# Attention scores: three products of rounded parts, or one product in whole fp32

## The chip, the cores and the metric

The kernel runs on one core of a Trainium2 chip. The core has a matrix engine (PE, TensorE; its weight loads are shown apart as PEld), a vector engine (DVE), an activation engine (ACT), a general engine (POOL, GpSimd) and a queue that issues DMAs (SP). Each follows its own stream of instructions in order and waits on semaphores. The metric is the device time of one launch in microseconds; lower is better.

## The reference

Sixteen graphs of 512 nodes with 64 channels each, and a dense 512x512 adjacency per graph, go through four residual layers, each behind a layer norm and a relu. The change concerns the second, a graph attention:

```
h1 = tanh(x @ enc_w + enc_b)
h2 = att_layer(h1, mask, ...)      # layer 1; h3 = att_layer(h2, mask, ...) is layer 2

def att_layer(h, mask, wv, bv, wk, bk, wq, bq):
    v = tanh(h @ wv + bv)
    q = tanh(h @ wq + bq)
    k = tanh(h @ wk + bk)
    scores = einsum('bnd,bmd->bnm', q, k)
    att = softmax(scores * mask - 9e15 * (1 - mask), axis=2)
    return einsum('bnm,bmd->bnd', att, v)

z = relu(concat(h2, h3) @ w1 + b1); z = relu(z @ w2 + b2); return z @ w3 + b3
```

Layer 0 is a Chebyshev graph convolution of order 4 (three products with the adjacency), layer 2 a normalised graph convolution, layer 3 one product with the adjacency. All values are fp32.

## The kernel before

**Graphs in a pipeline.** A round works on three graphs at once: the newest (age 0) in the Chebyshev layer, the one before (age 1) in attention, the oldest (age 2) in the end of attention's second layer, the MLP, the graph convolution and the last product. There are 18 rounds: three ahead of a loop, twelve in a loop of four turns with three rounds each, three behind it. Rounds 2 to 16 have a graph in both of the first two ages. The last two have no new graph.

**Order.** A table `ORDER` lists, for each engine, the steps of a round as `step.layer-age`; `walk` (L311) issues them in that order. Nothing is scheduled otherwise: an engine that waits in one step holds all steps behind it. The steps named below are those of this table. `mask0.1-1` is the mask of row block 0 in attention layer 1, for the graph of age 1.

**Attention on the engines.** A graph's 512 nodes are four blocks of 128 rows. For each of the two layers PE makes queries, keys and values (L1009, L1014, L1021 and L1025) one after another in one PSUM bank, `qkv_ps`. ACT takes each out with a tanh (L582, L596) before PE may write the next. Queries and keys are taken out twice: once into an fp32r tile, the rounded copy (`q_hi`, `k_hi`), and once whole into `q_t`, `k_t`. POOL subtracts the two (`split_qk`, L501) into the remainders `q_lo`, `k_lo`. A score block is then three fp32r matmuls added up in PSUM (L1040, L1043, L1044): `q_hi k_hi + q_hi k_lo + q_lo k_hi`. DVE multiplies it with the adjacency (L815) and adds the bias `gate` and takes the row's extreme (L821). `gate` is made by POOL in one operation over 128x2048, for each graph and each layer (`mask_bias`, L495). ACT makes the exponential (L605), PE transposes (L1058), ACT copies (L612), PE multiplies with the values (L1075, whole fp32 operands), DVE divides (L832).

**Around layer 1.** In PE's stream stand, from one graph to the next: `queries.1`, `turn_a0` (transposes of the next graph's adjacency, L917), two transposes of probabilities, `keys.1`, `turn_a1`, `spread_inv`, `values.1`, `turn_a2`, `turn_a3`, the previous graph's `attend.2`, then the score blocks. `turn_a2` and `turn_a3` write PSUM banks that DVE must first have read in `split_at0` and `split_at1` (L729). In DVE's stream these stand behind `norm_cheb`: a product (L715) and a copy (L723) of the normalised x. In POOL's stream `norm_cheb-0` is followed by `add_cheb_bias-0` (`x_b`, L439), `split_qk.1-1` and `mask_bias.1-1`.

**Around layer 2.** POOL has `norm_gcn-2`, `mask_bias.2-1`, `split_qk.2-1`, `cheb_f0-0` (L483 to L488), `norm_last-2`, `norm_enc-0`. DVE has `gcn_fold-2`, `stats_last-2`, `mask0.2-1`, `cheb_fold1-0`, `stats_enc-0`, `norm_last-2`, and PE's last product (L955 into `post_ps`) waits for the end of that. `norm_gcn` on DVE is L846 to L745, with the product L849.

Of the kernel before, what the change touches and what calls it, by code (L numbers as in the profile page):

```python
# [21 lines left out]
F32 = mybir.dt.float32  # L22
# [5 lines left out]
P = 128  # L28
# [29 lines left out]
    "gpsimd": """  # L58
        norm_cheb-0 add_cheb_bias-0 split_qk.1-1 mask_bias.1-1 inverse_roots-0 cheb_u3-0
        norm_gcn-2 mask_bias.2-1 split_qk.2-1 cheb_f0-0 norm_last-2 norm_enc-0  # L60
        add_mlp_bias-0""".split(),
# [35 lines left out]
def graph_layers(nc, x, adj, cheb_w, cheb_b, enc_w, enc_b, att_w, att_b, w1, b1, w2, b2, w3, b3,  # L97
# [11 lines left out]
    with ExitStack() as ctx:  # L109
        def sb(name, shape, dt=F32):  # L110
            return ctx.enter_context(nc.sbuf_tensor(name, shape, dt))

        def sem(name):
# [67 lines left out]
        c_diff = sb("c_diff", [P, RB, C])  # L181
        q_t, k_t = (sb(n, [P, N]) for n in ("q_t", "k_t"))
        v_n = [sb(f"v_n{a}", [P, N]) for a in range(2)]

        q_hi, k_hi, q_lo, k_lo = (
            [sb(f"{n}{a}", [P, N], F32R) for a in range(2)]
            for n in ("q_hi", "k_hi", "q_lo", "k_lo"))
        h1_t = sb("h1_t", [P, N])
# [88 lines left out]
        f0_done = sem("f0_done")  # L277
        qkv_split = sem("qkv_split")
        rstd_done = {t: sem(f"rstd_done_{t}") for t in ("pre", "post")}
# [129 lines left out]
        def _(pool):  # L409
# [87 lines left out]

            def split(whole, high, low, g, a, k):

                pool.wait_ge(qkv_done, 10 * g.n + 5 * a + 2 * k + 2)  # L500
                gp.tensor_tensor(low[a][:], whole[:], high[a][:].bitcast(F32), ALU.subtract)\  # L501
                    .then_inc(qkv_split, 1)

            def queries_keys(g, a):
                split(q_t, q_hi, q_lo, g, a, 0)
                split(k_t, k_hi, k_lo, g, a, 1)

            def add_mlp_bias(g):
# [14 lines left out]
                "add_mlp_bias": add_mlp_bias,  # L523
                **layer(0, split_qk=queries_keys, mask_bias=mask_bias),
                **layer(1, split_qk=queries_keys),
                **layer(1, mask_bias=mask_bias),
# [4 lines left out]
        def _(act):  # L531
# [44 lines left out]

            def take(g, a, k, whole, high, bias):

                for n, to in enumerate((high[a], whole)):
                    if n and follows(g, a):  # L580
                        act.wait_ge(qkv_split, 4 * g.n + 2 * a + k - 1)
                    sc.activation(to[:], qkv_ps[:], ACT.Tanh, **bias).then_inc(qkv_done, 1)  # L582

            def queries(g, a):
                if first(g) and a == 0:
                    act.wait_ge(weights_in, 16 * n_small)
                act.wait_ge(qk_ready, 4 * g.n + 2 * a + 1)
                take(g, a, 0, q_t, q_hi, {"bias": kq_bs[a][2][:]})

            def keys(g, a):  # L590
                act.wait_ge(qk_ready, 4 * g.n + 2 * a + 2)
                take(g, a, 1, k_t, k_hi, {"bias": kq_bs[a][1][:]})

# [310 lines left out]
        def _(pe):  # L904
# [94 lines left out]
            def queries(g, a):  # L999
                if first(g) and a == 0:  # L1000
                    pe.wait_ge(weights_in, 16 * n_small)
                if a == 0:
                    pe.wait_ge(h1_done, g.n + 1)
                else:
                    pe.wait_ge(attended, 2 * g.n + 1)
                if follows(g, a):

                    pe.wait_ge(qkv_done, 10 * g.n + 5 * a)
                te.matmul(qkv_ps[:], att_ws[a][2][:], source(g, a)[:], start=True, stop=True)\  # L1009
                    .then_inc(qk_ready, 1)  # L1010

            def keys(g, a):
                pe.wait_ge(qkv_done, 10 * g.n + 5 * a + 2)
                te.matmul(qkv_ps[:], att_ws[a][1][:], source(g, a)[:], start=True, stop=True)\  # L1014
                    .then_inc(qk_ready, 1)

            def values(g, a):
                if first(g) and a == 0:
                    pe.wait_ge(bias_rows, n_bias_rows)
                pe.wait_ge(qkv_done, 10 * g.n + 5 * a + 4)  # L1020
                te.matmul(qkv_ps[:], ones_bf[:, :],  # L1021
# [11 lines left out]
            def scores_rows(g, a, i):  # L1033
                if i >= 2 or follows(g, a):

                    pe.wait_ge(masked, 8 * g.n + 4 * a + i - 1)
                part = slice(i * P, (i + 1) * P)
                if i == 0:
                    pe.wait_ge(qkv_done, 10 * g.n + 5 * a + 3)
                te.matmul(score_ps[i % 2][:], q_hi[a][:, part], k_hi[a][:], start=True, stop=False)  # L1040
                if i == 0:
                    pe.wait_ge(qkv_split, 4 * g.n + 2 * a + 2)
                te.matmul(score_ps[i % 2][:], q_hi[a][:, part], k_lo[a][:], start=False, stop=False)  # L1043
                te.matmul(score_ps[i % 2][:], q_lo[a][:, part], k_hi[a][:], start=False, stop=True)\  # L1044
                    .then_inc(scores_ready, 1)
# [25 lines left out]
            def attend(g, a):  # L1071
                pe.wait_ge(qkv_done, 10 * g.n + 5 * a + 5)
                pe.wait_ge(pt_copied, 8 * g.n + 4 * a + 4)
# [91 lines left out]
```

## Time and profile before

| | |
|---|---|
| median of 3 timed runs | 913.66 us (913.12 to 913.68) |
| the profiled execution | 909.79 us |
| its span, first to last instruction | 908.0 us |
| PE busy | 775.2 us, 85% |
| DVE busy | 593.0 us, 65% |
| ACT busy | 447.5 us, 49% |
| POOL busy | 406.3 us, 45% |
| granted PE clock, mean | 0.973 of full |
| DMA | 24 GB/s over the span |

A busy share is a mean over the span and says which engine has the least room, not what it waits for. That is read from the timeline: a row gives the start, the duration, the engine, the line and the operands; "xN" counts the instructions of the row, and the bracket gives the idle time ahead of it and who ended it. An fp32 matmul shows as two records. Ends of PE's instructions are modelled, so the pace of a stream is read from one start to the next. Rows on POOL are rough in their ends.

### The profile page before, as it was taken

How to read it: one execution, taken by the hardware profiler on the slowest of the kernel's cores; microseconds unless marked ns; L12 is line 12 of the kernel's file. 1: busy time of each engine (PE TensorE's matmuls, PEld its weight loads, DVE VectorE, ACT ScalarE, POOL GpSimd, SP SyncE). 2: the span in 40 equal slices, each digit the busy share in tenths (PEclk: the TensorE clock that was granted, in tenths of full speed). 3: DMA queues.
4: the chain of work that ended last, by engine and by line, in shares of the span. 5: the costliest groups of instructions: out<-in, count | busy, mean ns of one | idle time of the engine just before them, and what ended most of it. 6: DMA issues, size and time to landing. Idle time of an engine off the chain costs nothing. (4 is left out here: it accounts for less than half of the span.)

```text
span 908.0 us, 13130 instructions
## 1 busy us (share of the span) xinstructions
PE 775.2 (85%) x3808; PEld 542.7 (60%) x3808; DVE 593.0 (65%) x1631; ACT 447.5 (49%) x929; POOL 406.3 (45%) x491
## 2 busy tenths in 40 slices
PE   3658798989999798989979898997989899898874
PEld 2435566666667566666756666664666666675543
DVE  3265677686776668677666767766776867765432
ACT  2044646547273644737364463736465472744430
POOL 3144545445553434555443455544454455533301
PEclk9869999999999999999999999999999999999996
DMA  5000101001020200101010010102010010000000
GB/s 170 32 1 1 52 1 40 20 1 59 1 59 0 60 0 6 53 0 58 0 59 0 12 46 0 58 0 59 0 49 9 0 58 0 6 2 6 1 6 6
DMA packets 29264, 22.54 MB, mean 25 GB/s; under 512 B 19488, under 2 KB 21024, under 8 KB 29216
## 3 DMA queue, kind: packets, MB, share of 16 engines
q1 hardware_dynamic: 29216, 22.03, 8.3%
q8 instruction: 14, 0.23, 0.1%
q14 instruction: 34, 0.28, 0.1%
HBM read 19.93 MB, written 2.10 MB: 24 GB/s over the span
## 5 line engine op out<-in xcount | busy, mean ns | idle before, releaser
L605 ACT ACTIVATE negz<-negz,negmax 128x512 f32<-128x512 f32 x128 | 92.3, 721 | 96.8 <-DVE negmax L821 95.7
L425 POOL TENSOR_TENSOR rstd_post<-vareps_post,nhalf 128x4 f32<-128x4 f32 x32 | 39.1, 1221 | 196.2 <-DVE vareps_post L708 196.2
L821 DVE CUSTOM_DVE_ANT_0 negz<-negz,gate 128x512 f32<-128x512 f32 x128 | 102.7, 802 | 23.8 <-DVE negz L815 23.6
L1075 PE MATMUL turn_ps<-pt,v_n 128*128 128x512 f32 x256 | 117.4, 602 | 0.0
L425 POOL TENSOR_TENSOR rstd_pre<-vareps_pre,nhalf 128x4 f32<-128x4 f32 x32 | 34.1, 1067 | 149.5 <-DVE vareps_pre L708 149.5
L955 PE MATMUL pre_ps<-at_hi,u_pair_pre 128*128 128x512 f32 x192 | 87.4, 455 | 7.4 <-DVE u_pair_pre L745 5.2
L815 DVE TENSOR_TENSOR negz<-score_ps,a_nat 128x512 f32<-128x512 f32 x128 | 88.0, 687 | 7.6 <-PE score_ps L1044 5.3
L955 PE MATMUL post_ps<-at_hi,u_pair_post 128*128 128x512 f32 x128 | 55.8, 436 | 38.4 <-DVE u_pair_post L745 38.4
L564 ACT ACTIVATE y_t_pre<-pre_ps 128x512 f32<-128x512 f32 x48 | 28.7, 597 | 118.4 <-PE pre_ps L955 117.6
L1058 PEld LDWEIGHTS turn_ps<-ident,negz 128*128 128x128 f32 x512 | 60.9, 141 | 33.7 <-ACT negz L605 14.6
L955 PE MATMUL pre_ps<-at_lo,u_pair_pre 128*128 128x512 f32 x192 | 78.5, 409 | 0.0
L1058 PE MATMUL turn_ps<-ident,negz 128*128 128x128 f32 x512 | 75.4, 274 | 2.9 <-ACT negz L605 2.7
L1075 PEld LDWEIGHTS turn_ps<-pt,v_n 128*128 128x128 f32 x256 | 47.2, 195 | 47.3 <-issue 47.3
L612 ACT ACTIVATE pt<-turn_ps 128x512 f32<-128x512 f32 x128 | 73.8, 590 | 1.0 <-PE turn_ps L1058 0.5
L501 POOL TENSOR_TENSOR k_lo<-k_t,k_hi 128x512 fp32r<-128x512 f32 x32 | 45.8, 1432 | 57.5 <-ACT k_t L582 57.5
L917 PE MATMUL pre_ps<-ident,a_nat 128*128 128x128 f32 x256 | 42.6, 299 | 25.5 <-DVE at_lo L729 17.8
L495 POOL TENSOR_SCALAR gate<-a_nat 128x2048 f32<-128x2048 f32 x32 | 60.8, 1899 | 4.2 <-DVE negmax L821 1.6
L1040 PE MATMUL score_ps<-k_hi,q_hi 128*128 128x512 f32 x128 | 61.5, 481 | 0.4 <-DVE negz L815 0.4
L917 PEld LDWEIGHTS pre_ps<-ident,a_nat 128*128 128x128 f32 x256 | 32.4, 151 | 48.0 <-issue 32.9
L501 POOL TENSOR_TENSOR q_lo<-q_t,q_hi 128x512 fp32r<-128x512 f32 x32 | 43.7, 1366 | 31.1 <-ACT q_t L582 31.1
L832 DVE TENSOR_TENSOR h_t<-turn_ps,inv_row 128x512 f32<-128x512 f32 x32 | 22.2, 693 | 53.2 <-PE turn_ps L1075 53.2
L729 DVE TENSOR_TENSOR at_lo<-pre_ps,at_hi 128x512 fp32r<-128x512 f32 x64 | 42.7, 685 | 20.5 <-ACT at_hi L537 20.5
(138 smaller groups left out, 1838.3 us busy)
## 6 DMA issues: line engine op xcount, KB each, us to landing
a_nat<-in_adj SPq DMA_DIRECT2D x16, 1024.0 KB, 5.7
x_in<-in_x SPq DMA_DIRECT2D x16, 128.0 KB, 2.3
out<-x_out SPq DMA_DIRECT2D x16, 128.0 KB, 1.9
cheb_ws<-in_L_gnn_weight SPq DMA_DIRECT2D x2, 64.0 KB, 5.0
att_w<-in_L_gnn_a_wv SPq DMA_DIRECT2D x2, 64.0 KB, 2.7
att_w<-in_L_gnn_a_wk SPq DMA_DIRECT2D x2, 64.0 KB, 2.5
att_w<-in_L_gnn_a_wq SPq DMA_DIRECT2D x2, 64.0 KB, 2.3
bv_f<-in_L_gnn_a_bv SPq DMA_DIRECT2D x2, 64.0 KB, 2.8
```

The costliest lines, as they stand in the source:

```text
L425: gp.tensor_tensor(rstd[t][:], vareps[t][:], nhalf[:, 0:RB], ALU.pow)\
L495: gp.tensor_scalar(gate[:], a_nat[g.slot][:], -1.0, NEG, ALU.add, ALU.mult)\
L501: gp.tensor_tensor(low[a][:], whole[:], high[a][:].bitcast(F32), ALU.subtract)\
L605: sc.activation(probs[:, i, :], negz[:, i, :], ACT.Exp, bias=negmax[:, i:i + 1], scale=-1.0, accum_out=total[:, i:i + 1]).then_inc(probs_d ...
L612: sc.activation(pt[:, :, i * P:(i + 1) * P], turn_ps[i % 2][:].rearrange("p (j n) -> p j n", n=P), ACT.Copy)\
L815: ve.tensor_tensor(negz[:, i, :], score_ps[i % 2][:], a_nat[s][:, i, :], ALU.mult)\
L821: ve.tensor_tensor_reduce(negz[:, i, :], negz[:, i, :], gate[:, i, :], -1.0, 3.0e38, ALU.add, ALU.min, negmax[:, i:i + 1]).then_inc(biased, 1)
L917: mm = te.transpose(pre_ps[:, j % 2, i * P:(i + 1) * P], a_nat[g.slot][:, i, j * P:(j + 1) * P], ident[:])
L955: mm = te.matmul(bank, u_pair[t][:, j, :, :].rearrange("p a c -> p (a c)"), at[g.slot][:, j, :], start=(j == 0 and at is at_hi), stop=(j = ...
L1040: te.matmul(score_ps[i % 2][:], q_hi[a][:, part], k_hi[a][:], start=True, stop=False)
L1058: mm = te.transpose(turn_ps[i % 2][:, j * P:(j + 1) * P], probs[:, i, j * P:(j + 1) * P], ident[:])
L1075: mm = te.matmul(turn_ps[0][:], v_n[a][:, j * P:(j + 1) * P], pt[:, j, :], start=(j == 0), stop=(j == RB - 1))
```

## The change

The rounded copies `q_hi`, `k_hi` and the remainders `q_lo`, `k_lo` are gone, and with them POOL's step `split_qk` in both layers and the semaphore `qkv_split`. ACT makes one tanh each for queries and keys, into `q_t` and `k_t`, which are now two buffers each (one per layer). A score block is one matmul of the whole fp32 tiles. The semaphore `qkv_done` counts three per layer and not five. No other step changes its place in any table.

```diff
     "gpsimd": """
-        norm_cheb-0 add_cheb_bias-0 split_qk.1-1 mask_bias.1-1 inverse_roots-0 cheb_u3-0
-        norm_gcn-2 mask_bias.2-1 split_qk.2-1 cheb_f0-0 norm_last-2 norm_enc-0
+        norm_cheb-0 add_cheb_bias-0 mask_bias.1-1 inverse_roots-0 cheb_u3-0
+        norm_gcn-2 mask_bias.2-1 cheb_f0-0 norm_last-2 norm_enc-0
         add_mlp_bias-0""".split(),
...
-            def split(whole, high, low, g, a, k):
-
-                pool.wait_ge(qkv_done, 10 * g.n + 5 * a + 2 * k + 2)
-                gp.tensor_tensor(low[a][:], whole[:], high[a][:].bitcast(F32), ALU.subtract)\
-                    .then_inc(qkv_split, 1)
...
-            def take(g, a, k, whole, high, bias):
-
-                for n, to in enumerate((high[a], whole)):
-                    if n and follows(g, a):
-                        act.wait_ge(qkv_split, 4 * g.n + 2 * a + k - 1)
-                    sc.activation(to[:], qkv_ps[:], ACT.Tanh, **bias).then_inc(qkv_done, 1)
-
...
-                take(g, a, 0, q_t, q_hi, {"bias": kq_bs[a][2][:]})
+                sc.activation(q_t[a][:], qkv_ps[:], ACT.Tanh, bias=kq_bs[a][2][:]).then_inc(qkv_done, 1)
...
-                take(g, a, 1, k_t, k_hi, {"bias": kq_bs[a][1][:]})
+                sc.activation(k_t[a][:], qkv_ps[:], ACT.Tanh, bias=kq_bs[a][1][:]).then_inc(qkv_done, 1)
...
             def values(g, a):
                 if first(g) and a == 0:
                     pe.wait_ge(bias_rows, n_bias_rows)
-                pe.wait_ge(qkv_done, 10 * g.n + 5 * a + 4)
+                pe.wait_ge(qkv_done, 6 * g.n + 3 * a + 2)
...
                 if i == 0:
-                    pe.wait_ge(qkv_done, 10 * g.n + 5 * a + 3)
-                te.matmul(score_ps[i % 2][:], q_hi[a][:, part], k_hi[a][:], start=True, stop=False)
-                if i == 0:
-                    pe.wait_ge(qkv_split, 4 * g.n + 2 * a + 2)
-                te.matmul(score_ps[i % 2][:], q_hi[a][:, part], k_lo[a][:], start=False, stop=False)
-                te.matmul(score_ps[i % 2][:], q_lo[a][:, part], k_hi[a][:], start=False, stop=True)\
+                    pe.wait_ge(qkv_done, 6 * g.n + 3 * a + 2)
+                te.matmul(score_ps[i % 2][:], q_t[a][:, part], k_t[a][:], start=True, stop=True)\
                     .then_inc(scores_ready, 1)
```

On POOL, in the round's first part, `rstd_pre` and `centred_pre` are `norm_cheb`, `x_b` is the bias added to x, `q_lo` and `k_lo` are the splits, and `rs` begins the inverse roots. Before:

```order
L425 TENSOR_TENSOR rstd_pre<-vareps_pre,nhalf 128x4
L428 TENSOR_TENSOR centred_pre<-x_in,meanvar_pre 128x256
L439 TENSOR_TENSOR x_b<-x_in,cheb_bs 128x256
L501 TENSOR_TENSOR q_lo<-q_t,q_hi 128x512
L501 TENSOR_TENSOR k_lo<-k_t,k_hi 128x512
L495 TENSOR_SCALAR gate<-a_nat 128x2048
L451 TENSOR_SCALAR rs<-rs 128x4
```

POOL in the same place now:

```order
L419 TENSOR_TENSOR rstd_pre<-vareps_pre,nhalf 128x4
L422 TENSOR_TENSOR centred_pre<-x_in,meanvar_pre 128x256
L433 TENSOR_TENSOR x_b<-x_in,cheb_bs 128x256
L489 TENSOR_SCALAR gate<-a_nat 128x2048
L445 TENSOR_SCALAR rs<-rs 128x4
```

The mask's bias has moved up by two operations and stands directly behind `x_b`.

On PE, from the attention product of the previous graph (L1075, now L1047) to the MLP: the score blocks 0, 1 and 2 of layer 1, with the transposes of the normalised x between. Before:

```order
L1075 MATMUL turn_ps<-pt,v_n 128x512 x4
L1040 MATMUL score_ps<-k_hi,q_hi 128x512
L1043 MATMUL score_ps<-k_lo,q_hi 128x512
L1044 MATMUL score_ps<-k_hi,q_lo 128x512
L927 MATMUL pre_ps<-ident,h_nat_pre 128x128 x4
```

PE in the same place now:

```order
L1047 MATMUL turn_ps<-pt,v_n 128x512 x4
L1016 MATMUL score_ps<-k_t,q_t 128x512
L903 MATMUL pre_ps<-ident,h_nat_pre 128x128 x4
L1016 MATMUL score_ps<-k_t,q_t 128x512 x2
L1056 MATMUL post_ps<-h_t,w_s 128x512
```

Every block has one matmul where it had three; nothing else on PE has moved.

## Rows read from the trace of the kernel before

**Rows 1.** The page, part 1: busy time, share of the span and instructions by engine.

```profile
PE 775.2 (85%) x3808; PEld 542.7 (60%) x3808; DVE 593.0 (65%) x1631; ACT 447.5 (49%) x929; POOL 406.3 (45%) x491
```

**Rows 2.** Windows of two rounds, encode to encode: length, busy (instructions), clock, DMA, GB/s.

```profile
303.54:359.05 55.51, 48.57 (x239) 34.01 (x239) 36.97 (x101) 27.95 (x59) 25.00 (x30) 0.97 0.08 24
...
409.90:461.09 51.19, 46.84 (x238) 33.10 (x239) 37.13 (x101) 27.79 (x59) 25.30 (x30) 1.00 0.09 26
```

**Rows 3.** Timeline of PE, one round: start, duration, line, operands, count, idle before.

```profile
416.65 0.39 PE L1021 MATMUL qkv_ps<-bv_rows,ones_bf 128*128 128x512 bf16 x1 [0.62 <-ACT k_t L582]
416.88 1.05 PE L1025 MATMUL qkv_ps<-att_w,h_t 128*128 128x128 f32 x8
418.21 1.25 PE L917 MATMUL pre_ps<-ident,a_nat 128*128 128x128 f32 x8 [0.28 <-DVE at_lo L729]
419.30 3.60 PE L1075 MATMUL turn_ps<-pt,v_n 128*128 128x512 f32 x8
```

**Rows 4.** Timeline of DVE: alone, then beside GpSimd's split and gate.

```profile
407.34 0.29 DVE L723 COPY h_nat_pre<-h_nat_pre 128x256 f32<-128x256 f32 x1
...
416.31 1.25 DVE L723 COPY h_nat_pre<-h_nat_pre 128x256 f32<-128x256 f32 x1
417.48 1.28 DVE L729 TENSOR_TENSOR at_lo<-pre_ps,at_hi 128x512 fp32r<-128x512 f32 x2
...
440.94 2.02 DVE L849 SCALAR_TENSOR_TENSOR u<-centred_post,rstd_d 128x256 f32<-128x256 f32 x1
```

**Rows 5.** Timeline of POOL (GpSimd), same round.

```profile
415.27 0.72 POOL L439 TENSOR_TENSOR x_b<-x_in,cheb_bs 128x256 f32<-128x256 f32 x1
415.95 1.45 POOL L501 TENSOR_TENSOR q_lo<-q_t,q_hi 128x512 fp32r<-128x512 f32 x1
...
440.79 1.90 POOL L495 TENSOR_SCALAR gate<-a_nat 128x2048 f32<-128x2048 f32 x1
```

**Rows 6.** Timeline of ACT: the second tanh of the keys, layer 1.

```profile
415.87 0.72 ACT L582 ACTIVATE k_t<-qkv_ps,kq_b 128x512 f32<-128x512 f32 x1
```

**Rows 7.** Timeline of PE: score block 2, layer 1, then two fp32 matmuls.

```profile
424.56 0.40 PE L1040 MATMUL score_ps<-k_hi,q_hi 128*128 128x512 f32 x1
...
425.26 1.02 PE L1084 MATMUL post_ps<-h_t,w_s 128*128 128x512 f32 x2
426.12 1.02 PE L1085 MATMUL post_ps<-h_t,w_s 128*128 128x512 f32 x2
```

**Rows 8.** Timeline of PE: projection of the Chebyshev weights in two rounds.

```profile
270.49 0.33 PE L943 MATMUL pre_ps<-cheb_hi,h_t 128*128 128x192 f32 x1
...
428.02 0.33 PE L943 MATMUL pre_ps<-cheb_hi,h_t 128*128 128x192 f32 x1 [0.45 <-DVE h_t L737]
```

**Rows 9.** Timeline of DVE: graph convolution's statistics and first mask of layer 2.

```profile
450.26 0.67 DVE L708 TENSOR_SCALAR vareps_post<-meanvar_post 128x4 f32<-128x4 f32 x1
...
451.89 1.05 DVE L821 CUSTOM_DVE_ANT_0 negz<-negz,gate 128x512 f32<-128x512 f32 x1 [0.18 <-DVE negz L815]
```

**Rows 10.** Last two rounds: PE, with its waits.

```profile
829.94 1.12 PE L1014 MATMUL qkv_ps<-h_t,att_w 128*128 128x512 f32 x2 [0.48 <-ACT q_t L582]
...
832.42 0.39 PE L1021 MATMUL qkv_ps<-bv_rows,ones_bf 128*128 128x512 bf16 x1 [0.80 <-ACT k_t L582]
...
860.39 0.50 PE L1043 MATMUL score_ps<-k_lo,q_hi 128*128 128x512 f32 x1 [1.63 <-POOL k_lo L501]
```

**Rows 11.** Timelines of POOL and DVE, last two rounds: split, first mask of layer 2.

```profile
858.80 1.54 POOL L501 TENSOR_TENSOR k_lo<-k_t,k_hi 128x512 fp32r<-128x512 f32 x1 [2.98 <-ACT k_t L582]
...
861.23 0.69 DVE L815 TENSOR_TENSOR negz<-score_ps,a_nat 128x512 f32<-128x512 f32 x1 [0.64 <-PE score_ps L1044]
```

**Rows 12.** Timeline of PE where the loop turns.

```profile
314.77 1.68 PE L917 MATMUL pre_ps<-ident,a_nat 128*128 128x128 f32 x8 [2.63 <-DVE at_lo L729]
316.24 4.91 PE L1075 MATMUL turn_ps<-pt,v_n 128*128 128x512 f32 x8
```

**Rows 13.** Window of one microsecond in that place; PEclk is the granted clock.

```profile
316.00:317.00 1.00, 1.00 (x4) 0.58 (x3) 0.69 (x1) 1.00 (x4) 1.00 (x1) 0.50 0.00 0
```

More of the change, by code:

```diff
@@ L181, in graph_layers @@
         c_diff = sb("c_diff", [P, RB, C])
[L182 to L187, printed above, removed]
+        q_t, k_t, v_n = ([sb(f"{n}{a}", [P, N]) for a in range(2)] for n in ("q_t", "k_t", "v_n"))
         h1_t = sb("h1_t", [P, N])
@@ L277, in graph_layers @@
         f0_done = sem("f0_done")
-        qkv_split = sem("qkv_split")
         rstd_done = {t: sem(f"rstd_done_{t}") for t in ("pre", "post")}
@@ L496, in mask_bias @@
                     .then_inc(gate_done, 1)
-            def split(whole, high, low, g, a, k):
-                pool.wait_ge(qkv_done, 10 * g.n + 5 * a + 2 * k + 2)
-                gp.tensor_tensor(low[a][:], whole[:], high[a][:].bitcast(F32), ALU.subtract)\
-                    .then_inc(qkv_split, 1)
-            def queries_keys(g, a):
-                split(q_t, q_hi, q_lo, g, a, 0)
-                split(k_t, k_hi, k_lo, g, a, 1)
             def add_mlp_bias(g):
@@ L523, in _ @@
                 "add_mlp_bias": add_mlp_bias,
-                **layer(0, split_qk=queries_keys, mask_bias=mask_bias),
-                **layer(1, split_qk=queries_keys),
+                **layer(0, mask_bias=mask_bias),
                 **layer(1, mask_bias=mask_bias),
@@ L1006, in queries @@
                 if follows(g, a):
-                    pe.wait_ge(qkv_done, 10 * g.n + 5 * a)
+                    pe.wait_ge(qkv_done, 6 * g.n + 3 * a)
                 te.matmul(qkv_ps[:], att_ws[a][2][:], source(g, a)[:], start=True, stop=True)\
@@ L1012, in keys @@
             def keys(g, a):
-                pe.wait_ge(qkv_done, 10 * g.n + 5 * a + 2)
+                pe.wait_ge(qkv_done, 6 * g.n + 3 * a + 1)
                 te.matmul(qkv_ps[:], att_ws[a][1][:], source(g, a)[:], start=True, stop=True)\
@@ L1071, in attend @@
             def attend(g, a):
-                pe.wait_ge(qkv_done, 10 * g.n + 5 * a + 5)
+                pe.wait_ge(qkv_done, 6 * g.n + 3 * a + 3)
                 pe.wait_ge(pt_copied, 8 * g.n + 4 * a + 4)
```

## The prediction, made before the changed kernel was run

> **What bounds the kernel now.** The page first: PE is busy 85% of the span, DVE 65%, ACT 49%, POOL 45% [rows 1]. So only what PE does, or waits for, can move the end much; work on ACT and POOL is worth nothing in itself. Then the rounds, cut at each encoder matmul: a plain round lasts about 51.2 us with 46.84 us of PE work, and three rounds in which the loop turns last up to 55.5 us [rows 2]. PE therefore idles about 4.3 us in a plain round. The timeline of PE shows where: before the values it waits 0.62 us for ACT's second tanh of the keys, then 0.28 us for DVE before the last two transposes of the next adjacency [rows 3]. Of the rest, 0.45 us in some rounds before the Chebyshev weights is for DVE too [rows 8]; the others are DVE work of the other graphs.
>
> The end is thus set by PE and, in turns, by the chain of DVE and POOL that feeds it. The changed kernel is read the same way: which wait ends last at each of these places.
>
> **PE's own work.** Three fp32r matmuls of a score block take 0.70 us (from 424.56 to 425.26); one fp32 matmul of the same 128x512 shape takes 0.86 us (from 425.26 to 426.12), the record count x2 being its two parts [rows 7]. So a block becomes 0.16 us dearer where it stood back to back. Behind transposes the fp32r block already took 0.78, so there it is 0.08; behind an fp32r product an fp32 matmul takes 0.91, which makes 0.20 for block 3 of layer 1. Per round that is +0.17 (behind the attention product), +0.08, +0.16 and +0.20 in layer 1. Layer 2's blocks are +0.1 or less each; PE then waits for DVE or ACT anyway (1.3 us before the last propagation), so they are covered. Bounds of one block: 0 (its wait for the remainder goes) and 0.20.
>
> How much of layer 1 shows? Blocks 0 to 2 stand between the attention product of the previous graph and the Chebyshev weights. In eight rounds of fifteen PE reaches the weights without a wait; there 0.17 + 0.08 + 0.16 = 0.41 is paid. In seven PE waits some 0.45 us for DVE [rows 8]; there only what DVE sees is paid: mask 0 started as block 0 ended, and so starts 0.18 later. Block 3 adds 0.20 in each, since PE is without a wait from there until the graph convolution's product. Sum: 8 x 0.61 + 7 x 0.38 = **+7.5 us**.
>
> **The second tanh and the wait for it.** 64 ACTIVATEs of 0.7 us go. Keys and values of layer 1 are chained through one PSUM bank, so PE's values can start when the keys' first tanh is done: where the second starts now, at 415.9 rather than at 416.65 [rows 3, 6]. PE gains 0.7 us there, if nothing is late next. Layer 2's projections are spread between long products and gain nothing.
>
> **What is late next.** The transposes at 418.21 already wait for DVE. They need its first difference, which is queued behind the copy of the normalised x. That copy takes 0.29 us alone and 1.25 us here [rows 4]: it started at 416.31 while POOL ran the split of the queries, from 415.95 to 417.40 [rows 5], and it ended 0.16 us behind it. So a copy on DVE gets nowhere while POOL runs a big operation. With the splits gone, what POOL has next is the mask's bias `gate` over 128x2048, until now behind both splits. Its waits are long fulfilled, so it follows `x_b` directly. It takes 1.90 us, and DVE's product beside it took 2.02 us instead of its usual 0.42 [rows 4, 5]. The split took 1.30 us when nothing held it, so the copy is held 1.90 - 1.30 = **0.60 us longer**. The differences then start at 418.1 and not at 417.48, the transposes at 418.8, the attention product at 419.9 and not at 419.30. PE's 0.7 us gained at the values turn into a longer wait here (values end at about 417.2; idle some 1.6 us). This happens in 15 rounds: 15 x 0.60 = **+9.0 us**. Bounds of this term: 0 for each, if the copy is held only as long as beside a split (1.25 us), and 0.75, if it ends as far behind the gate as the 2.02 us row did. I take 0.60, by both rows together. The Trainium skill, "SBUF — State Buffer", "Who interferes with whom", says that a copy in a two-port mode and a GpSimd instruction take turns on one port pair, and that the one that comes second is fully blocked till the other ends. By that rule the term stands at the gate's whole length, with the row of the graph convolution; by the 1.25 us row alone it would be nil and the sum 9.0 us lower.
>
> **POOL elsewhere.** In layer 2 the splits delayed `cheb_f0` and with it the root of the last normalisation. `c_diff` held DVE's tiny addition (0.67 us, 0.17 alone), and further POOL work held the first mask's second half (1.05 us, 0.69 alone) [rows 9]. With the splits gone the first goes, but mask 0 then waits for its scores, which are no earlier. The second shrinks by about 0.2: the centring then ends near 452.1 where now the hold ends at 452.35. DVE is without a wait from there to the last propagation, on which PE waits. So 14 x -0.2 = **-2.8 us**.
>
> **The last two rounds** have no next graph, so nothing else fills the waits and no normalisation stands beside the gate. Layer 1: PE's 0.48 and 0.80 us for ACT's tanhs go, some 1.15 us with their tails [rows 10]; score blocks take back 0.3. Layer 2: PE stands 1.63 us for the keys' split of 1.54 us, behind a tanh of 0.6 [rows 10, 11]. Scores would be ready near 859.4 and not at 861.18, so DVE's mask can start when its own work ends, at 860.6, not at 861.23; the blocks behind run at full clock instead of half, and the last propagation starts some 2 us earlier. Together **-2.9 us**.
>
> **Sum.** 7.5 + 9.0 - 2.8 - 2.9 = +10.8 us on the profiled execution's 909.8 us, which is 920.6. The median of the timed runs is 913.66, 3.9 above the profiled one; with the same offset the forecast is **924.5 us**.
>
> **Rivals.**
> 1. *The copy slips in ahead of the gate.* DVE's product before it ends at 416.28, and if POOL's gate were issued after that, the copy would be done by 416.6. The values' gain would then stay: transposes at 417.23 behind the values, attention product at 418.4, 0.9 earlier than now. 15 x -0.9 + 7.5 - 2.8 - 2.9 = -11.7, about 902 us. Against it: at this same place the split, issued at 415.95 behind `x_b`, went first in every round [rows 5]. 0.13. The Trainium skill, "SBUF — State Buffer", "Who interferes with whom", also says that the order of issue decides who is blocked, and that is this rival's condition.
> 2. *The hold does not lengthen with the gate.* Then the 9.0 us go, 915.5. 0.10.
> 3. *The clock falls in the longer wait.* Where the loop turns PE idled 2.63 us at this place, and the granted clock fell to 0.50, the 1.2 GHz level: the attention product took 4.91 us instead of 3.60 and the transposes 1.68 instead of 1.25 [rows 3, 12, 13]. That is 1.7 us an event. In plain rounds the clock stayed at 1.00, the 2.4 GHz level, with idle stretches of up to 1.3 us. A new stretch of 1.6 us lies between. If half of the twelve plain rounds fall, +10, 935 us; if all, 945. It decides from one round upward. 0.17.
> 4. *Everything is covered*, +-1.8 us: only if the fp32 blocks cost nothing and rival 2 holds. 0.05.
>
> **How the numbers follow.** The forecast has 0.55. Its own range is 917 to 931: the hold term from 0 to 0.75 each and the block term with half its size either way. To hold 8 in 10 the range takes in rival 2 and half of rival 3: 911 to 938. Left out are rival 1 and the far end of rival 3. A measurement here can tell about 0.2%, 1.8 us. Faster by more: rival 1 and a little of 2, 0.15. Within: 0.06. Slower: 0.79.
>
> **What would show it.** On the changed kernel's timeline: one fp32 score matmul (x2) of 0.86 us pitch; `gate` directly behind `x_b`; DVE's copy beside it 1.8 us or more, not 1.25; PE's wait before the last adjacency transposes 1.5 us, its wait before the values gone; a plain round of 51.8 to 52.2 us instead of 51.2; the last scores of layer 2 without a wait. A copy of 0.29 us at that place would prove rival 1, a clock below 1.00 in plain rounds rival 3. The forecast fails as a whole if PE's wait there is not longer than now, or if the fp32 matmul runs at another pace than its neighbours.

## The result, and the profile after

The changed kernel takes **928.94 us** (median of four runs, 926.40 to 933.42); the kernel before took 913.39 us in the runs beside it. The ratio is 1.0177, 95% interval 1.0137 to 1.0218: slower by 15.5 us. Forecast were 924.5 us and a range of 911 to 938. Direction and range held; the sum behind them had the largest mechanism right, some of its sizes wrong, and a rival happened beside the forecast.

The page of the changed kernel, part 1 and two groups of part 5 (line, engine, operands, count; busy us and mean ns; idle before them and its main releaser), answers to [rows 1]:

```profile
PE 790.9 (85%) x3648; PEld 525.9 (57%) x3680; DVE 592.0 (64%) x1631; ACT 413.2 (45%) x865; POOL 312.2 (34%) x427
...
L1016 PE MATMUL score_ps<-k_t,q_t 128*128 128x512 f32 x256 | 127.9, 602 | 0.0
...
L893 PE MATMUL pre_ps<-ident,a_nat 128*128 128x128 f32 x256 | 43.4, 304 | 46.2 <-DVE at_lo L705 38.3
```

POOL lost 94 us of work and ACT 34, and the kernel is longer all the same. PE's busy time rose by 15.7 us, which is not all scores: where the granted clock is low, the same matmuls last longer. The real rise is some 7 us larger, because this trace has no record of the values' bias matmul (L1021 in [rows 3], 32 of them, 0.23 us each from its start to the next one's). The group to look at is the last. PE stood idle for 46.2 us ahead of the adjacency's transposes, 38.3 of them for DVE's `at_lo`; in the kernel before it was 25.5 and 17.8:

```profile
L917 PE MATMUL pre_ps<-ident,a_nat 128*128 128x128 f32 x256 | 42.6, 299 | 25.5 <-DVE at_lo L729 17.8
```

Timelines of one plain round (clock 1.00 throughout), DVE, POOL, ACT and PE, which answer to [rows 3 to 6]:

```profile
426.18 0.93 DVE L691 SCALAR_TENSOR_TENSOR h_nat_pre<-centred_pre,rstd_pre 128x256 f32<-128x256 f32 x1 [1.64 <-POOL centred_pre L422]
427.15 1.87 DVE L699 COPY h_nat_pre<-h_nat_pre 128x256 f32<-128x256 f32 x1
428.94 1.27 DVE L705 TENSOR_TENSOR at_lo<-pre_ps,at_hi 128x512 fp32r<-128x512 f32 x2
```

```profile
426.10 0.73 POOL L433 TENSOR_TENSOR x_b<-x_in,cheb_bs 128x256 f32<-128x256 f32 x1
426.92 1.95 POOL L489 TENSOR_SCALAR gate<-a_nat 128x2048 f32<-128x2048 f32 x1
```

```profile
425.87 0.70 ACT L568 ACTIVATE k_t<-qkv_ps,kq_b 128x512 f32<-128x512 f32 x1
```

```profile
426.85 1.05 PE L1001 MATMUL qkv_ps<-att_w,h_t 128*128 128x128 f32 x8 [0.30 <-ACT k_t L568]
429.67 1.25 PE L893 MATMUL pre_ps<-ident,a_nat 128*128 128x128 f32 x8 [1.76 <-DVE at_lo L705]
...
430.75 3.60 PE L1047 MATMUL turn_ps<-pt,v_n 128*128 128x512 f32 x8
434.19 1.02 PE L1016 MATMUL score_ps<-k_t,q_t 128*128 128x512 f32 x2
435.05 0.60 PE L903 MATMUL pre_ps<-ident,h_nat_pre 128*128 128x128 f32 x4
```

Read them across. `gate` starts at 426.92, directly behind `x_b`; the copy starts 0.23 us after it and ends at 429.02, 0.15 us after `gate` (before, it ended 0.16 after the split [rows 4, 5]). PE's values (L1001, before L1025) start 6.13 us after the round's encode, 0.85 earlier than before, and this turns into idle time: 1.76 us before the transposes. The 0.30 us of idle time shown before the values includes the unrecorded bias matmul of 0.23 us. The attention product starts 10.03 us after the encode, before 9.40 [rows 2, 3].

Windows from encode to encode (length; busy time and instructions by engine; granted clock, DMA share, GB/s): two plain rounds, and one where the loop turns [rows 2]:

```profile
205.84:259.49 53.65, 48.75 (x228) 32.33 (x231) 37.01 (x101) 25.68 (x55) 19.19 (x26) 0.97 0.09 25
311.19:368.66 57.47, 50.20 (x229) 33.38 (x231) 37.03 (x101) 25.77 (x55) 18.86 (x26) 0.94 0.08 24
420.72:472.39 51.67, 47.17 (x228) 31.76 (x231) 36.71 (x101) 25.70 (x55) 19.57 (x26) 1.00 0.08 26
```

The first is a plain round in which the clock fell, which the kernel before never showed in its plain rounds. PE there, and two single microseconds (last but two numbers: clock):

```profile
214.88 1.25 PE L893 MATMUL pre_ps<-ident,a_nat 128*128 128x128 f32 x8 [1.85 <-DVE at_lo L705]
215.97 5.29 PE L1047 MATMUL turn_ps<-pt,v_n 128*128 128x512 f32 x8
```

```profile
215.00:216.00 1.00, 1.00 (x9) 0.82 (x10) 0.42 (x1) 0.43 (x1) 0.00 (x0) 1.00 0.05 16
...
217.00:218.00 1.00, 1.00 (x2) 0.33 (x1) 0.69 (x1) 1.00 (x3) 0.00 (x0) 0.50 0.00 0
```

After 1.85 us without work the transposes still run at 1.00, the 2.4 GHz level; then the clock falls to 0.50, the 1.2 GHz level, and the attention product takes 5.29 us instead of 3.60. That is 1.69 us, as much as rival 3 had priced one event.

So the 19.7 us between the two profiled executions (908.0 and 927.7 us of span) fall into:

| Stretch | before | after | difference |
|---|---|---|---|
| to the first encode | 52.42 | 53.92 | +1.50 |
| first two rounds | 98.80 | 100.24 | +1.44 |
| seven plain rounds, clock 1.00 | 356.74 | 362.58 | +5.84 (0.83 each) |
| three plain rounds in which the clock fell after | 153.03 | 160.64 | +7.61 (2.54 each) |
| three rounds where the loop turns | 164.97 | 169.33 | +4.36 |
| from the last encode | 82.04 | 80.99 | -1.05 |

### The profile page after: what moved, and what is told of

It is laid out like the page before. It is cut to its first block and busy times, and to the rows that moved or that the text cites. A ratio compares the mean times of both kernels' runs of the same rounds, so it can differ in the third digit from the quotient of the medians.

```text
span 927.7 us, 12634 instructions
## 1 busy us (share of the span) xinstructions
PE 790.9 (85%) x3648; PEld 525.9 (57%) x3680; DVE 592.0 (64%) x1631; ACT 413.2 (45%) x865; POOL 312.2 (34%) x427
## 5 line engine op out<-in xcount | busy, mean ns | idle before, releaser
L1016 PE MATMUL score_ps<-k_t,q_t 128*128 128x512 f32 x256 | 127.9, 602 | 0.0
L419 POOL TENSOR_TENSOR rstd_post<-vareps_post,nhalf 128x4 f32<-128x4 f32 x32 | 32.8, 1025 | 274.8 <-DVE vareps_post L684 274.8
L1047 PE MATMUL turn_ps<-pt,v_n 128*128 128x512 f32 x256 | 124.2, 631 | 0.0
L893 PE MATMUL pre_ps<-ident,a_nat 128*128 128x128 f32 x256 | 43.4, 304 | 46.2 <-DVE at_lo L705 38.3
L1047 PEld LDWEIGHTS turn_ps<-pt,v_n 128*128 128x128 f32 x256 | 49.7, 204 | 51.8 <-issue 51.8
L520 ACT ACTIVATE at_hi<-pre_ps 128x512 fp32r<-128x512 f32 x64 | 38.4, 600 | 44.6 <-PE pre_ps L893 44.5
L1016 PEld LDWEIGHTS score_ps<-k_t,q_t 128*128 128x128 f32 x256 | 43.9, 192 | 25.2 <-issue 17.0
```

The source lines that it names most:

```text
L419: gp.tensor_tensor(rstd[t][:], vareps[t][:], nhalf[:, 0:RB], ALU.pow)\
L893: mm = te.transpose(pre_ps[:, j % 2, i * P:(i + 1) * P], a_nat[g.slot][:, i, j * P:(j + 1) * P], ident[:])
L1016: te.matmul(score_ps[i % 2][:], q_t[a][:, part], k_t[a][:], start=True, stop=True)\
L1047: mm = te.matmul(turn_ps[0][:], v_n[a][:, j * P:(j + 1) * P], pt[:, j, :], start=(j == 0), stop=(j == RB - 1))
```

## The experiments

The theory: POOL's `gate` holds DVE's copy for its whole length (0.60 us a round more than the split did), fp32 score blocks cost some 0.5 us a round, and the longer wait of PE sometimes brings the clock down. The rivals: the fp32 blocks alone are the cost, or the clock alone. "Plain" below is the mean of the same ten plain rounds of the profiled execution (before 50.98 us; the changed kernel 52.32, and 51.80 in its seven without a fall). Ratios are to the kernel before on the same chip.

| Run | median us | ratio (95% interval) | plain | wait for `at_lo` |
|---|---|---|---|---|
| changed kernel | 928.94 | 1.0177 (1.0137 to 1.0218) | 52.32 | 1.8 to 2.0 |
| 1: gate behind the copy | 898.52 | 0.9831 (0.9784 to 0.9877) | 50.30 | 0.2 to 0.5 |
| 2: before, gate ahead of the splits | 923.93 | 1.0139 (1.0089 to 1.0188) | 51.45 | 0.9 to 1.2 |
| 3: before, fp32 block alone | 913.49 | 1.0010 (0.9986 to 1.0034) | 51.38 | 0.3 to 0.6 |
| 4: changed, work in the wait | 918.45 | 1.0060 (1.0042 to 1.0079) | 51.84 | 0 to 0.3 |
| 5: changed, gate ahead | 901.97 | 0.9873 (0.9844 to 0.9903) | 50.32 | 0.2 to 0.5 |
| 6: changed, gate ahead, bias late | 896.36 | 0.9823 (0.9801 to 0.9846) | 49.99 | 0 |
| 7: before, all behind the copy | 903.43 | 0.9900 (0.9879 to 0.9922) | 50.55 | 0 to 0.2 |
| 8: fp32 block, no second splits | 914.42 | 1.0025 (1.0012 to 1.0039) | 51.23 | 0.3 to 0.6 |
| 9: changed, wait and bias late | 894.60 | 0.9799 (0.9775 to 0.9822) | 50.00 | 0 |
| 10: changed, gate in halves | 908.98 | 0.9955 (0.9939 to 0.9971) | 50.88 | 0.9 to 1.2 |

**1. The gate behind the copy.** One wait is added to the changed kernel.

```diff
             def mask_bias(g, a):
+                if a == 0 and not (isinstance(g.n, int) and g.n == B - 1):
+                    pool.wait_ge(h_ready["pre"], 2 * (g.n + 1) + 1)
                 if follows(g, a):
```

> The changed kernel; POOL's mask bias of layer 1 waits until DVE has made the copy of the normalised x, so that the two cannot overlap. Theory A (POOL's gate holds DVE's copy, the fp32 blocks cost 0.16 us each, and the long wait now and then drops PE's clock): the copy takes 0.3 us and not 1.87, PE's wait before the last adjacency transposes goes, the attention product of a plain round starts some 1.5 us earlier, the clock stays at 1.00 in plain rounds. 15 x -1.5 and some -7 us of clock: about 899 us, faster than both kernels. Theory B (the slowdown is the fp32 matmuls' price alone): within 2 us of the changed kernel's 929. A middle case, in which another wait takes the place of the one removed, would be 910 to 920.

Measured: 898.52 us. DVE, then POOL, in the same place:

```profile
414.23 0.29 DVE L701 COPY h_nat_pre<-h_nat_pre 128x256 f32<-128x256 f32 x1
414.44 1.28 DVE L707 TENSOR_TENSOR at_lo<-pre_ps,at_hi 128x512 fp32r<-128x512 f32 x2
```

```profile
414.80 1.90 POOL L491 TENSOR_SCALAR gate<-a_nat 128x2048 f32<-128x2048 f32 x1 [0.89 <-DVE h_nat_pre L701]
```

The copy takes 0.29 us, and no plain round has a fall of the clock. Shifting one operation of an engine that is busy a third of the time is worth 3.4% of the run. Without the hold the changed kernel is 1.7% faster than the kernel before, which still has its own; experiment 7 compares the two with the hold out of both.

**2. The hold alone.** The kernel before, with two steps of POOL's order exchanged, so that `gate` and not the split meets the copy.

```diff
-        norm_cheb-0 add_cheb_bias-0 split_qk.1-1 mask_bias.1-1 inverse_roots-0 cheb_u3-0
+        norm_cheb-0 add_cheb_bias-0 mask_bias.1-1 split_qk.1-1 inverse_roots-0 cheb_u3-0
```

> The kernel before with its three products; only the order of two steps on POOL is changed: the gate of layer 1 stands ahead of the splits instead of behind them. Theory A: the copy is held for the gate's 1.9 us instead of the split's 1.3, which is 0.60 us in each of 15 rounds, 913.4 + 9.0 = 922.4 us, without a fall of the clock in plain rounds, since PE's wait there is 0.9 us only. Theory B: no difference, 913 us.

Measured: 923.93 us (Theory A had 922.4), with the three fp32r products and both tanhs in place. DVE and POOL:

```profile
423.61 1.87 DVE L723 COPY h_nat_pre<-h_nat_pre 128x256 f32<-128x256 f32 x1
```

```profile
423.38 1.96 POOL L495 TENSOR_SCALAR gate<-a_nat 128x2048 f32<-128x2048 f32 x1
425.41 1.27 POOL L501 TENSOR_TENSOR q_lo<-q_t,q_hi 128x512 fp32r<-128x512 f32 x1
```

1.87 us, as in the changed kernel, and PE's wait there is 0.6 us longer. Of that 0.46 us a round shows in nine plain rounds: in some of them the wait before the Chebyshev weights [rows 8], 0.45 us, is gone in exchange. The other microseconds of this run are not in its profiled execution, which was the shortest of its four (918.96 of up to 928.39); they vary from run to run, as in the changed kernel.

**3. The fp32 block alone.** The kernel before with all tanhs and splits kept; what the splits make is unread, and `q_t` and `k_t` are two buffers each, as in the changed kernel.

```diff
-                te.matmul(score_ps[i % 2][:], q_hi[a][:, part], k_hi[a][:], start=True, stop=False)
...
-                te.matmul(score_ps[i % 2][:], q_hi[a][:, part], k_lo[a][:], start=False, stop=False)
-                te.matmul(score_ps[i % 2][:], q_lo[a][:, part], k_hi[a][:], start=False, stop=True)\
+                te.matmul(score_ps[i % 2][:], q_t[a][:, part], k_t[a][:], start=True, stop=True)\
```

> The kernel before with both tanhs, both splits and all waits of ACT and POOL kept; only PE's score block is one fp32 matmul of the whole queries and keys and does not wait for the splits, whose results nothing reads any more. Theory A: +7.5 us for the blocks, less some 1.7 us in the last round, where PE no longer waits for the split: 913.4 + 5.8 = 919 us; a plain round of 51.4 to 51.7 us. Theory B: the whole difference, 929 us.

Measured: 913.49 us, no difference that can be told, and 5.5 us under the expected 919. Its plain rounds did grow, by 0.40 us: by 0.58 in the six in which PE had no wait before the Chebyshev weights (forecast 0.61), by 0.13 in the four that had one (forecast 0.38). In the profiled execution its three loop turns gave 2.5 us of that back: they took up to 54.2 us each, where the kernel before took up to 55.7, with two falls of the clock. Whether the other executions behind the median did the same is not shown. PE at one such place:

```profile
317.57 1.25 PE L916 MATMUL pre_ps<-ident,a_nat 128*128 128x128 f32 x8 [2.63 <-DVE at_lo L728]
318.66 3.60 PE L1070 MATMUL turn_ps<-pt,v_n 128*128 128x512 f32 x8
```

The same 2.63 us of idle time that had brought the clock down before [rows 12] did not here, in any of the three turns. In the kernel before itself the third turn had no fall either. The length of the idle stretch alone does not decide; what else does, these runs do not show.

**4. Work in the long wait.** The changed kernel with seven fp32r matmuls ahead of the last transposes, into a score bank that is written anew afterwards.

```diff
+                        if j == 2 and follows(g):
...
+                            for _ in range(7):
+                                te.matmul(score_ps[0][:], ident_r[:], at_hi[g.slot][:, 0, :],
+                                          start=True, stop=True)
                         pe.wait_ge(at_split, 4 * g.n + j - 1)
```

> The changed kernel with seven fp32r matmuls of 128x512 that compute nothing of use, on PE ahead of the last two adjacency transposes, where PE waits 1.8 us. They end before that wait does, or about with it. If the falls of the granted clock come from this wait, they vanish in the plain rounds and where the loop turns the second fall goes as well: three to four plain rounds and two of the turns lose 1.9 us each, 919 to 922 us, and the spread of the runs shrinks. If the clock has nothing to do with that wait: 929 us, with long rounds as before.

Measured: 918.45 us, just under the expected 919 to 922. PE, and two windows, one plain round and one turn:

```profile
420.58 1.87 PE L895 MATMUL score_ps<-at_hi,ident_r 128*128 128x512 f32 x7
422.59 1.25 PE L899 MATMUL pre_ps<-ident,a_nat 128*128 128x128 f32 x8
```

```profile
203.21:255.29 52.08, 48.84 (x235) 32.94 (x237) 37.11 (x101) 25.68 (x55) 19.59 (x26) 1.00 0.09 26
...
306.96:361.55 54.59, 49.02 (x236) 32.96 (x238) 36.87 (x101) 25.80 (x55) 19.55 (x26) 1.00 0.09 25
```

The transposes come no earlier, and undisturbed plain rounds are as long as they were (51.7 and 52.1 us). In the profile only the rounds with a fall are gone: useless work made the kernel 1.2% shorter, some 10 us of the 15.5, and the spread of its ten runs is 3.0 us, that of the changed kernel's four 7.0. Part of this is falls in the turns, which the kernel before has too.

**5. The gate ahead of everything.** No wait, another place in the order.

```diff
-        norm_cheb-0 add_cheb_bias-0 mask_bias.1-1 inverse_roots-0 cheb_u3-0
+        mask_bias.1-1 norm_cheb-0 add_cheb_bias-0 inverse_roots-0 cheb_u3-0
```

> The changed kernel with one word moved in POOL's written order: the mask's bias `gate` is put ahead of `norm_cheb` and the bias sum `x_b`, and so runs in POOL's idle stretch before the normalisation rather than beside DVE's copy of the normalised x. No wait is added. Theory (the copy is held only because the 1.9 us operation is issued just before it): as with the gate behind the copy, the long wait before the adjacency transposes is gone and the time is about 899 us, 895 to 903; the copy takes 0.3 us, and PE's wait for `at_lo` stays under 0.6 us. Rival (moving the gate merely moves the hold to DVE's statistics ahead of the copy, which then come later by up to 1.6 us): 910 to 929 us.

Measured: 901.97 us, within the theory's 895 to 903, plain rounds as in experiment 1 (50.32 and 50.30), the copy 0.29 us. So it is the place, not the wait. The first encode came at 56.01 us and the third at 155.40, in experiment 1 at 54.15 and 151.58; the 3.4 us between their spans lie there, 1.9 of them ahead of the first encode, where `gate` has not run yet and both kernels issue the same work.

**6. The bias sum moved too.** POOL's `x_b` behind `cheb_u3`.

```diff
-        mask_bias.1-1 norm_cheb-0 add_cheb_bias-0 inverse_roots-0 cheb_u3-0
+        mask_bias.1-1 norm_cheb-0 inverse_roots-0 cheb_u3-0 add_cheb_bias-0
```

> The same kernel with `add_cheb_bias` (POOL's sum `x_b`) moved as well, behind `cheb_u3`, so that no large operation of POOL stands beside DVE's difference, product and copy of the normalisation. Theory (every large POOL operation costs DVE its own length there): DVE's product beside `x_b` falls from 0.93 to 0.42 us, the differences start 0.5 us earlier; PE's wait for `at_lo` can shrink by the 0.2 to 0.5 us that were left with the gate behind the copy, so 15 x 0.2 to 0.5 = 3 to 7 us less than with the gate ahead alone: 892 to 896 us. Rival (PE is bound by its own values product there, or `x_b` is then late for the first Chebyshev product): no gain or some us slower, 898 to 905 us.

Measured: 896.36 us, 0.4 above the expected 892 to 896 and below the rival's 898. DVE and PE:

```profile
416.03 0.43 DVE L691 SCALAR_TENSOR_TENSOR h_nat_pre<-centred_pre,rstd_pre 128x256 f32<-128x256 f32 x1 [1.65 <-POOL centred_pre L422]
416.49 0.29 DVE L699 COPY h_nat_pre<-h_nat_pre 128x256 f32<-128x256 f32 x1
```

```profile
416.70 1.05 PE L1001 MATMUL qkv_ps<-att_w,h_t 128*128 128x128 f32 x8
417.59 1.36 PE L893 MATMUL pre_ps<-ident,a_nat 128*128 128x128 f32 x8
```

DVE's product falls from 0.93 to 0.43 us: it too had been held, by `x_b`. PE has no wait left at this place, and a plain round is 0.33 us shorter.

**7. Three products without the hold.** The kernel before, its splits and gate behind the copy.

```diff
             def queries_keys(g, a):
+                if a == 0 and not (isinstance(g.n, int) and g.n == B - 1):
+                    pool.wait_ge(h_ready["pre"], 2 * (g.n + 1) + 1)
```

> The kernel before (three fp32r products, both splits) with POOL made to wait, ahead of layer 1's splits, for DVE's copy of the newer graph's normalised x. Splits and gate then run behind the copy. Theory (POOL's large operation holds DVE's copy, whichever it is): the copy falls from 1.25 to 0.3 us, PE's wait for `at_lo` (0.28) goes, and the first scores' remainders come 0.4 us later, which they can afford: 913 minus 15 x 0.3 to 0.6, 904 to 909 us. Beside the changed kernel with its gate behind the copy (898.5) it tells what the edit itself brings once the hold is gone in both: by my theory the edit then gains, by 6 us or more. Rival (the splits are late for the scores or for ACT's tanh of the next layer, which waits for them): 913 to 925 us.

Measured: 903.43 us, just under the expected 904 to 909. Beside experiment 1 it prices the edit itself, with the hold out of both: ratios 0.9900 and 0.9831, plain rounds 50.55 and 50.30. By the ratios one fp32 product is the better code by about 6 us, but only where the operation behind the splits is kept off the copy; the two intervals almost touch (from 0.9879, and up to 0.9877). The spans of the two profiled executions differ by 5.5 us, of which 2.5 lie in the ten plain rounds and 3.0 in the first two rounds.

**8. Layer 2's splits left out,** on top of experiment 3. Nothing reads them there.

```diff
             def split(whole, high, low, g, a, k):
+                if a == 1:
+                    return
```

> The kernel before with one fp32 product per score block (as in the run that changed the block alone: 913.5 us), and with layer 2's two splits left out, whose results nothing reads there; layer 1's splits and all second tanhs stay. It measures the term `POOL elsewhere`, forecast at 14 x -0.2 = -2.8 us, and what the end gains by it. Theory: 910.7 us, 908 to 912, since DVE's tiny addition of the graph convolution is no longer held. Rival (mask and normalisation have slack there, or something else of POOL's takes the split's place beside DVE): 913.5 us, 912.5 to 915.

Measured: 914.42 us; no gain against experiment 3, rather the rival's number. In its profile the plain rounds are 0.15 us shorter, near the 0.2 forecast, but two of its three turns had a fall of the clock (164.3 us together against 162.5), and the whole is no shorter. The term exists in the rounds and does not reach the median here.

**9. The best of both.** The wait of experiment 1, and `x_b` behind `cheb_u3`.

> The changed kernel with the wait that puts `gate` behind DVE's copy of the normalised x, and with POOL's bias sum `x_b` moved behind `cheb_u3`, so that neither stands beside DVE's product and copy. Theory: the steady rounds of the run with gate and bias sum moved (50.2, 49.9, and 52.8 us where the loop turns) with the start of the run that only had the wait (the third encoder matmul at 151.6 us and not at 157.8): 889 to 892 us. Rival (the gain of that run came from the gate's place ahead of the normalisation, which also took away the 0.3 us at the values): 894 to 898 us.

Measured: 894.60 us. Its plain rounds are those of experiment 6 (50.00 and 49.99), and the first encode comes at 53.54 us, not at 57.04, with the same work ahead of it in both. But the two rounds behind it take 100.7 us in both, and 97.4 in experiment 1. The third encode comes at 154.26, the expected 151.6 was wrong, and the time is the rival's 894 to 898 and not 889 to 892. The rival's reason is not borne out: the plain rounds are equal, and its 0.3 us at the values is for the most part the bias matmul, which has no record in this trace and has one in that of experiment 6. Nor is the slow start shown to belong to the bias sum's new place: the second round takes 51.9 us at a mean clock of 0.95 in experiment 5 and 51.9 at 0.94 in experiment 10, where the bias sum stands in its old place, as it takes 52.1 at 0.94 here, against 49.6 at 1.00 in experiment 1. A low clock goes with it, and its cause stays open. This version beats both kernels, by 2.0% the one before and by 3.7% the changed one.

**10. The gate in two halves,** back to back.

```diff
-                gp.tensor_scalar(gate[:], a_nat[g.slot][:], -1.0, NEG, ALU.add, ALU.mult)\
+                gp.tensor_scalar(gate[:, :RB // 2], a_nat[g.slot][:, :RB // 2], -1.0, NEG, ALU.add, ALU.mult)
+                gp.tensor_scalar(gate[:, RB // 2:], a_nat[g.slot][:, RB // 2:], -1.0, NEG, ALU.add, ALU.mult)\
```

> The changed kernel with `gate` written by two instructions over two row blocks each (128x1024), one directly behind the other, in place of one over 128x2048. It asks what the hold follows: one POOL instruction, or POOL's being busy at all. Theory A (DVE's copy waits for the end of the one instruction that holds it, and is served before POOL's next): copy about 1.0 to 1.2 us and not 1.87, PE's wait for `at_lo` about 1.0 us and not 1.8, 15 x 0.8 = 12 us less and no falls of the clock in plain rounds (some 5 us more): 908 to 917 us. Theory B (POOL's second instruction follows its first without a gap and the copy waits for both): 1.9 us or slightly more, 928 to 931 us.

Measured: 908.98 us, within Theory A's 908 to 917. DVE, then POOL:

```profile
419.00 1.02 DVE L700 COPY h_nat_pre<-h_nat_pre 128x256 f32<-128x256 f32 x1
```

```profile
418.77 1.10 POOL L489 TENSOR_SCALAR gate<-a_nat 128x1024 f32<-128x1024 f32 x1
419.93 1.05 POOL L490 TENSOR_SCALAR gate<-a_nat 128x1024 f32<-128x1024 f32 x1
```

The copy ends 0.15 us after the first half (0.14 or 0.15 in all fifteen rounds), when by its record the second has been under way for 0.09 us. It waits for one instruction, not for POOL to be idle. The same work cut in two, at the same place, takes 2.2% off the changed kernel: PE idles 0.9 us there, and no plain round has a fall.

The Trainium skill, "SBUF — State Buffer", "Who interferes with whom", says of a DVE instruction in a two-port mode and one of GpSimd that the one issued first keeps the shared ports for its whole length and that the other is blocked meanwhile. The runs agree, with 1.87 us beside 1.95 and 1.02 beside 1.10; that the blocked one waits for a single instruction and not for the next one right behind it is what experiment 10 adds.

## Why the prediction came out as it did

**The hold on the copy, +9.0 us: right.** Forecast were a copy of 1.8 us or more, a wait of 1.5 us and an attention product 0.60 later; measured were 1.87, 1.76 and 0.63. Where the loop turns, and PE had no wait for ACT to lose, the wait grew from 2.63 to 3.26 us, by 0.63 again. Experiment 2 made the same 1.87 without the rest of the edit, experiments 1 and 5 removed it. Of the two rows that bounded the term, the 2.02 us beside the gate [rows 4, 5] was the right one. In the seven plain rounds without a fall the edit can be followed step by step: the fp32 block alone makes +0.39 us a round (experiment 3), leaving out the second splits -0.19 (experiment 8), and the way from there to the changed kernel +0.64, which is the hold, with the values' gain lost in it. Forecast were 0.50, -0.19 and 0.60. Made first, as in experiment 2, the hold shows as 0.46 only, since it then uses up the wait before the Chebyshev weights [rows 8] that otherwise the block uses up: that wait can be spent once.

**The values' gain, turned into idle time: right.** PE starts them 0.85 us earlier, and all of it is lost before the transposes. The wait that was to be gone is gone but for some 0.07 us, an estimate: the 0.30 us shown less the 0.23 us of the unrecorded bias matmul. Experiments 3 and 8 bear it out: the same two tanhs show 0.84 us without that record and 0.62 with it.

**The fp32 block, +7.5 us: mechanism right, size too large.** Measured 0.40 us a round, some 6 us. The step that was mis-sized is "there only what DVE sees is paid": in rounds where PE had waited before the Chebyshev weights, 0.13 us was paid and not 0.38. The wait took nearly all of it.

**POOL elsewhere, -2.8 us: size near, small.** 0.15 us a round in experiment 8, which is some 2 us, and not visible in its median. Hold, block and this term together gave 0.91 a round in the forecast; the undisturbed plain rounds grew by 0.83. Those without a wait before the Chebyshev weights grew by 1.09 (forecast 1.01), those with one by 0.50 (forecast 0.78), so the sum was too high where the wait before the weights took up what was added.

**The last two rounds, -2.9 us: right until the clock took half back.** From the last encode to the graph convolution's product 0.82 us were gained, from there to the last product's propagation 1.58 (9.86 us, before 11.44). The next thing late was POOL: `centred_post` held DVE for half a microsecond, so it was not the full 2. Timeline of DVE there:

```profile
880.44 0.69 DVE L791 TENSOR_TENSOR negz<-score_ps,a_nat 128x512 f32<-128x512 f32 x1
881.30 0.69 DVE L797 CUSTOM_DVE_ANT_0 negz<-negz,gate 128x512 f32<-128x512 f32 x1 [0.17 <-DVE negz L791]
...
882.50 0.43 DVE L691 SCALAR_TENSOR_TENSOR h_nat_post<-centred_post,rstd_post 128x256 f32<-128x256 f32 x1 [0.50 <-POOL centred_post L422]
```

Then 1.35 us went back at the very end, 0.87 of it where the eight small matmuls of the graph convolution ran at the low clock (1.97 us, before 1.10). Net -1.05.

**Rival 3, the clock: it happened beside the forecast.** I gave it 0.17 as a case of its own. It was a surcharge on the forecast: three of ten plain rounds fell, at about 1.6 us each, near the price of 1.7, some 5 us together (53.65 and 53.63 us beside 52.07 in undisturbed rounds of the same kind). "If half of the twelve plain rounds fall, +10" was the right kind of sum with too many events. The turns grew by 4.36 us, where 0.83 to 0.91 a round give 2.5 to 2.7. Two of the three had a fall in either kernel, but before each cost 1.7 to 1.9 us and now 2.9 to 3.0 (57.47 and 57.36 us beside 54.49); one price for an event does not hold. By experiment 4 the falls were worth about 10 us in the medians. Two readings of the trace before were incomplete: the longest turn took 55.7 us and not 55.5, and in the third PE idled 2.64 us without a fall, which speaks against the rival's plain "the clock fell".

**Rivals 1, 2 and 4 did not happen.** The copy never came ahead of `gate` (rival 1), and the hold was as long as `gate` (rival 2).

**The sum: nearer than its terms, by luck.** It was built on the profiled execution, and there the change is +19.7 us, not +10.8. Of the 8.9 us missing, by the table above, the ten plain rounds make 4.4 (falls +5, less what the block fell short), the turns 1.6, the last rounds 1.9 and the start 1.5, while the first two rounds took 0.4 less than forecast. The medians are only 4.4 us apart because the prediction added the 3.9 us by which the old kernel's median lay above its profiled execution; the changed kernel's median lies 0.55 below its own. Had I costed the clock as a term (a few events at 1.7 us or more, in the direction of every longer wait), the forecast would have been nearer for its reasons too. The start is left open: the first encode came between 52.3 and 57.0 us over the kernels of this study, and between 52.3 and 56.0 over the ten that do the same until there, so the 1.5 us belong to no step of the edit.

## What to carry to other kernels

When work is taken off an engine, ask what runs there next, and what it then runs beside: here POOL lost 94 us and the kernel became 15.5 us slower, because a longer POOL instruction slid beside a DVE copy of 0.29 us that PE waited for. Look for short DVE copies and products whose duration follows that of a POOL neighbour; keep them apart by order or by a wait, or cut the long instruction. And where PE's wait grows, even by time that PE had just saved elsewhere, put a price on falls of its clock: neither their number nor their size was fixed here (1.0 to 3.0 us each), so both can only be bounded.

## What the hardware showed beyond this

- DVE's copy, begun beside a POOL instruction, ends a fixed time behind that one, whichever it is: 0.14 to 0.16 us behind the split, the whole gate and the half one, in all fifteen rounds of each of the seven profiles that have the hold. DVE's two-operand products have the same behaviour with another offset: 0.28 us behind `x_b` (0.93 us instead of 0.43), 0.27 behind layer 2's gate [rows 4, 5].
- The same idle stretch of PE gives different clocks: 2.63 us with a fall before [rows 12, 13] and without one in experiment 3, and in the changed kernel 3.26 us twice with a fall and once without (PE's timeline, two of the three turns of the loop):

```profile
323.01 1.97 PE L893 MATMUL pre_ps<-ident,a_nat 128*128 128x128 f32 x8 [3.26 <-DVE at_lo L705]
324.77 5.67 PE L1047 MATMUL turn_ps<-pt,v_n 128*128 128x512 f32 x8
...
484.09 1.25 PE L893 MATMUL pre_ps<-ident,a_nat 128*128 128x128 f32 x8 [3.26 <-DVE at_lo L705]
485.18 3.60 PE L1047 MATMUL turn_ps<-pt,v_n 128*128 128x512 f32 x8
```

  In the ten plain rounds none had a fall where the wait was 1.2 us or less, in any kernel profiled here, and three of ten where it was 1.8 to 2.0. Where the loop turns, the profiles without filler work had a fall behind 0 of 5 waits of 1.5 us, 3 of 10 of 2.0, 2 of 3 of 2.4, 4 of 9 of 2.6 and 4 of 6 of 3.3.
- A fall shows in the work behind the idle stretch, sooner or later: in the plain round the transposes still ran at 1.00 and only the product was at 0.50; in the turn at 323 us the transposes were slow already (1.97 us instead of 1.25).
